# One scatter and one gather moved a step later in a batch, and the opening's identity products sent to another bank

## The reference

```python
x = x + L0_xcond(layernorm(x), ctx, ctx, tau, delta, Wq..bo)   # 16 heads of 16
x = x + L0_ffn(layernorm(x), router, 64 experts, top 8, shared expert)
x = x + L1_xcond(layernorm(x), ctx, ctx, tau, delta, Wq..bo)
x = x + L1_ffn(layernorm(x), router, 8 experts, top 2)

# xcond: scores = (q k^T) * tau + delta; a = softmax(scores / 4); out = (a v) Wo^T + bo
# ffn:   every chosen expert: silu(x Wg) * (x Wu) Wd, times the routing weight, summed per row
```

## Time and profile before

| | us |
|---|---|
| median of 3 runs | 1405.54 |
| lowest and highest run | 1402.01, 1406.44 |
| the profiled execution, its time | 1418.99 |
| its span | 1417.3 |
| PE busy in it | 1272.4 (90% of the span) |
| DVE, ACT, POOL busy | 827.8, 492.7, 557.1 |
| granted TensorE clock, mean | 0.928 |

### The profile page before, as it was taken

The page is one execution under the profiler, slowest core; times in us unless marked ns, Lnnn a source line. Parts: engine busy times, 40 slices in busy tenths (PEclk is TensorE's granted clock), DMA queues, the critical chain, the costliest instruction groups (busy, mean ns, idle before and its releaser), DMA issues. The chain is left out here.

```text
span 1417.3 us, 40365 instructions
## 1 busy us (share of the span) xinstructions
PE 1272.4 (90%) x12838; PEld 980.2 (69%) x12839; DVE 827.8 (58%) x2642; ACT 492.7 (35%) x1255; POOL 557.1 (39%) x706
## 2 busy tenths in 40 slices
PE   5999898999966999999848999999999989999996
PEld 3666565666643788888635666666666779999995
DVE  3467766666746666666445666776676354444442
ACT  1454444344421243344214444444344212212221
POOL 2135555454444101100355655666552223332322
PEclk9999999898977999999967988999899699999998
DMA  4334444335532667875322332333321512533423
GB/s 113 105 110 133 124 131 123 121 115 171 157 118 67 210 201 228 249 221 159 109 76 63 86 87 72 95 90 91 82 68 44 189 40 39 156 93 100 127 66 78
DMA packets 115804, 166.65 MB, mean 118 GB/s; under 512 B 26480, under 2 KB 96768, under 8 KB 114672
## 3 DMA queue, kind: packets, MB, share of 16 engines
q0 software_dynamic: 22672, 58.41, 16.2%
q1 hardware_dynamic: 46496, 54.35, 13.2%
q10 hardware_dynamic: 46560, 52.98, 11.6%
HBM read 87.82 MB, written 63.49 MB: 107 GB/s over the span
## 5 line engine op out<-in xcount | busy, mean ns | idle before, releaser
L1047 DVE TENSOR_REDUCE mx<-banks 112x2 f32<-112x750 f32 x256 | 235.7, 936 | 137.0 <-PE banks L627 111.5
L1894 POOL DMA_INDIRECT xs_d<-xns,idx x160 | 155.1, 969 | 176.6 <-PE banks L651 130.6
L1567 ACT ACTIVATE shared_buf<-banks 125x672 f32<-125x672 f32 x256 | 173.0, 727 | 104.1 <-PE banks L651 94.5
L651 PE MATMUL banks<-attn_buf 18*125 18x112 f32 x3072 | 135.2, 301 | 43.9 <-DVE mx L1047 32.2
L1908 POOL DMA_INDIRECT kept<-y_d,yidx x128 | 123.6, 965 | 119.8 <-issue 91.0
L651 PEld LDWEIGHTS banks<-attn_buf 18*125 18x125 f32 x3072 | 109.8, 198 | 74.3 <-DVE mx L1047 36.7
L919 PEld LDWEIGHTS banks<-xT,attn_buf 128*128 128x128 f32 x1364 | 157.1, 192 | 5.1 <-DVE xT L1433 3.6
L919 PE MATMUL banks<-xT,attn_buf 128*128 128x128 f32 x1364 | 157.4, 275 | 3.3 <-DVE xT L1433 3.3
L864 PE MATMUL banks<-xT,staged 128*128 128x128 f32 x1064 | 142.8, 277 | 6.8 <-DVE staged L1444 6.5
L864 PEld LDWEIGHTS banks<-xT,staged 128*128 128x128 f32 x1064 | 129.1, 192 | 11.5 <-DVE xT L1433 8.1
L627 PE MATMUL banks<-attn_buf 17*112 17x375 f32 x1024 | 123.4, 553 | 7.6 <-ACT shared_buf L1567 7.3
(11 more groups left out here) (214 smaller groups left out, 1957.2 us busy)
## 6 DMA issues: line engine op xcount, KB each, us to landing
shared_buf<-xs_d SPq DMA_DIRECT2D x136, 128.0 KB, 2.5
y_d<-shared_buf ACTq DMA_DIRECT2D x132, 128.0 KB, 2.6
ringbuf<-in_we SPq DMA_DIRECT2D x6, 2176.0 KB, 8.2
ringbuf<-in_we POOLq DMA_DIRECT2D x32, 384.0 KB, 4.7
attn_buf<-attn_buf SPq DMA_DIRECT2D x128, 93.8 KB
attn_buf<-in_ctxT ACTq DMA_DIRECT2D x29, 375.0 KB
xs_d<-zrow ACTq DMA_DIRECT2D x16, 512.0 KB
y_d<-zrow ACTq DMA_DIRECT2D x16, 512.0 KB
```

Source lines behind the costliest of these rows:

```text
L651: last = pe.matmul(bank[SCORES_T[j]][0:KT, t * Q:(t + 1) * Q], kT4[rows, u, i, t * KT:(t + 1) * KT], qT4[rows, u, i, :], start=True, stop= ...
L1047: dve.tensor_reduce(mx[:, i % 2, 2 * p:2 * p + 2], banks[0:Q, 2 * p:2 * p + 2, 0:S], AX.X, ALU.max).then_inc(s_max, 1)
L1567: act.activation(pT[:, slot:slot + 2, :], banks[0:KT, first_bank:first_bank + 2, 0:ST * Q], ACT.Exp, scale=0.25).then_inc(s_exp, 1)
L1894: pool.indirect_dma_start(xs_d[L.number], bass.IndirectOffsetOnAxis(ap=idx[:, b % 2, k:k + 1], axis=0), rows, None).then_inc(s_scat[b % 2] ...
```

## The change

Three edits:

- FILL makes 8 identity products in place of 10, writes bank 4 (the first of the `scores_T` banks) in place of bank 7, and no longer waits for bank 7 to be free.
- In layer 0, POOL's step 0 has one scatter in place of two (k = 2), its step 1 three in place of two (k = 3, 4, 5).
- In layer 1, POOL's step 0 has no gather, its step 1 four in place of three.

```diff
-        FIRST_JOBS = ((... ("ROW1", 0), ("MAX", 0), ("FILL", 10)),
+        FIRST_JOBS = ((... ("ROW1", 0), ("MAX", 0), ("FILL", 8)),
...
                         elif j == "FILL":
-                            for sm, v in free[1]:
-                                wait(pe, sm, v)
-                            idle(r, M1)
+                            idle(r, bank[SCORES_T[0]])
...
                 def body0(n, b):
                     after_scores(n, 0)
                     if in_layer(b, -3):
-                        scatter(L, n - 3, b - 3, 2, 2)
+                        scatter(L, n - 3, b - 3, 2, 1)
                     after_scores(n, 1)
                     if in_layer(b, -3):
-                        scatter(L, n - 3, b - 3, 4, 2)
+                        scatter(L, n - 3, b - 3, 3, 3)
                     if in_layer(b, -1):
                         normalise(1, n - 1, b - 1)
...
                     if in_layer(b, 4):
                         output_row_numbers(b + 4, b % 2)
-                        gather(b + 4, b % 2, 0, 1)
                     after_scores(n, 1)
                     if in_layer(b, 4):
-                        gather(b + 4, b % 2, 1, 3)
+                        gather(b + 4, b % 2, 0, 4)
                     if in_layer(b, -1):
                         normalise(1, n - 1, b - 1)
```

More of the change, by code:

```diff
@@ L318, in build @@
         SP_ATTN, SP_TAB, SP_LATE, SP_PACK, SP_ROWS, SP_LAST, SP_OPEN = (0, 39), (18, 57), 19, 20, 21, (25, 30, 36), 37
-        FIRST_JOBS = ((("K0", 0), ("V2", 0), ("K1", 0), ("XT", 0), ("Q", 0), ("XT", 1), ("V01", 0), ("K0", 1), ("K1", 1), ("ROW0", 0), ("Q", 1), ("BO", 0), ("ROW1", 0), ("MAX", 0), ("FILL", 10)),
+        FIRST_JOBS = ((("K0", 0), ("V2", 0), ("K1", 0), ("XT", 0), ("Q", 0), ("XT", 1), ("V01", 0), ("K0", 1), ("K1", 1), ("ROW0", 0), ("Q", 1), ("BO", 0), ("ROW1", 0), ("MAX", 0), ("FILL", 8)),
                       (("UP3", 0), ("XT", 0), ("Q", 0), ("DOWN3", 0), ("ROW0", 0), ("XT", 1), ("Q", 1), ("ROW1", 0), ("MAX", 0), ("BO", 0)))
```

## The result

| us | before | after |
|---|---|---|
| median of 4 runs | 1405.99 | 1424.93 |
| lowest and highest | 1402.01, 1412.38 | 1419.58, 1426.05 |
| profiled execution, its span | 1417.3 | 1417.9 |
| PE busy in it | 1272.4 | 1280.8 |
| granted clock in it | 0.928 | 0.921 |

The ratio after to before is 1.012, 95% interval 1.0079 to 1.016: the change makes the kernel **slower, by about 17 us**. The forecast was 12 us faster. The two profiled executions have equal spans, because the one of before was slower than each of its four runs (1418.99 against a highest of 1412.38) and the one of after was its fastest. So the profiles are read by place, not by their sum.

The account below looks back on a forecast made before the run. PE was taken to fill the span, so only PE's waits counted. Terms -3.8 (opening), -9.4 (layer 0) and +1.0 (layer 1) gave -12.2 us: 1406.8 profiled, 1393 as run median; range 1382 to 1404.

Parts of the forecast that it names:

- Opening: Start of the program: identity products no longer wait for bank 7, so batch 0's score rows start 3.8 us earlier.
- Layer 0, step 0: Batches 4 to 11: one scatter fewer ends the late signals to DVE; 9.4 us gained, bounds 0 and 9.4.
- the maxima start when DVE is free: Layer 0, batches 4 to 11: DVE's first maxima instruction of step 1 starts 1.2 us earlier, and PE's scores with it.
- Layer 0, step 1. ... Cost nothing: The moved scatter takes 1.25 us ahead of POOL's layer norm chain, covered by 1.71 us of idle time; no cost.
- the rival: Layer 0: third scatter delays step 2's signals; 1409 us, or 1418 if step 1 keeps its stall; chance 0.13.
- the sum: Total of the terms for opening, layer 0 and layer 1: 12.2 us faster, chance 0.40.
- Batch 12: Layer 0: a second scatter lies over the score rows' end, yet the maxima follow without pause; basis for a zero lower bound.
- 1.0 us lost: Layer 1, step 1: the added gather makes xn2 late for PE by 0 to 0.47 us in four batches; middle taken.
- where no row shows that anybody waits for it; I count no gain: Layer 1, step 0: taking the gather out of this step was counted as worth 0 us.
- half clock going away with the pauses: Layer 0, step 1: full clock returns once PE no longer stands, 8.6 us more, 1385 us in all; chance 0.15.

Follow-up runs that it names:

- the written-out loop: Kernel before the change, with DVE's loop over batches 4 to 11 of layer 0 written out except batches 6 and 7; ratio to before 0.9948.
- the three moves of a gather: Against before: fourth gather in step 1 (1.0062), or one gather moved from step 1 to step 0 (1.0085); changed kernel, gather behind layer norm's chain (1.0046 to before).

## Why the prediction was wrong

**Opening: right.** 3.8 us expected, 4.0 by the rows; that products which serve nobody held up the program is shown. Alone it measures 0.9921, 11 us; more than its 4 us, since layer 0's clock was better as well (0.97 against 0.94). How much of that belongs to the edit the profiles can't say, and so the match of 3.8 and 4.0 is one of the rows and not of the ratio.

**Layer 0, step 0: the stall went, its gain did not.** The step "the maxima start when DVE is free" came true. The failed step is the next one, "Layer 0, step 1. ... Cost nothing". I costed the third scatter by its effect on POOL's own chain, and did not put it beside the score rows of step 2, although the rival did exactly that, with the right times. I gave it only 0.13, arguing that a signal at the scatter's end would cost nothing; it came 0.94 us behind that end. PE's wait is 0.86 us at batch 8, not 1.2, so by its waits alone the edit still paid: PE stands 5.9 us less in batches 4 to 11. The second step that failed is the clock, which the sum held as it was: PE is busy 12.7 us longer there, at 0.88 in place of 0.95. Net 365.0 against 365.9, and 1.0038 (0.9990 to 1.0086) alone. Batch 12, my reason for doubt, was no evidence against a scatter as the cause: when the moved scatter stood behind the layer norm's chain, the scatters had all but left the rows' end in steps 0 to 2 of batches 4 to 11, no signal was late there, and the stage ran 19 to 24 us shorter than in before, 9 to 13 shorter than with the opening's edit alone. That is more than the earlier trace rows could give, since the late signals of step 0 went as well, and all half clock of these batches. Why batch 12 was spared is still open, like the odd batches of the written-out loop.

**Layer 1: the largest error.** "1.0 us lost" came from xn2 alone, with bounds 0 and 1.9; the attention went from 387.6 to 404.1 us. On the chip of the forecast this term was nothing: in batches 2 to 13 PE never waits for xn2, before or after. Where nothing else disturbs, it is 5.5 us, above its bound, since PE waits in 11 batches and not in four. The step that failed is "where no row shows that anybody waits for it; I count no gain", and with it that the gather costs nothing at its new place but xn2. PE stands in `scores_T` while a gather is issued, at the old place (2.24 us in place of 0.92 in batch 4, step 1) and at the new one (1.54 in step 2). I had looked for it in no row of layer 1, though I had seen the same coincidence in layer 0. These holds nearly balance; what the move brought is mostly half clock, 8.8 of 11.3 us in batches 4 to 11. That the gather's edit makes the kernel slower is shown by the runs of the parts, and that its loss needs a chip with stalls by the 1.002 on one without; that half clock is the link is read from one profile of before and two of the changed kernel.

**The clock** went against me in both layers. I gave 0.15 to half clock going away with the pauses, named as a point against it that a shifted program may bring half clock elsewhere, and put a price on the first alone.

The range, 1382 to 1404, ended below the measured 1424.93: I had left the one slower rival outside it, and even that one's 1418 had no more than the 1.0 us for layer 1.

## What to carry to other kernels

Before a DMA of POOL is moved, draw where its issue lies against PE's groups, at the old place and the new, in every layer that has such DMAs; each of the three moves of a gather tried here on a chip with stalls freed one meeting and made another. Only the order that took the scatters off the end of the score rows in steps 0 to 2 was worth something. And time a candidate on more than one chip: an edit may buy only what one chip loses.

## What the runs showed of the hardware

- While POOL issues an indirect DMA (0.93 to 0.97 us each in the rows above), on some chips PE's work beside it is held: signals of score rows arrive up to 1.2 us late at DVE, and groups of transposed scores that take 0.92 us take 1.5 to 2.2 at full clock, with pauses of 0.2 to 0.4 us inside them. With 16 rows in place of 112 the pause inside was 0.24 us in place of 0.26.
- On other chips of the same type the same overlap costs nothing: the group takes 0.92 us under a gather of 0.93, the maxima start 0.18 us behind the rows' end under a scatter of 0.94. The whole kernel is 7% faster there, 1312 against 1409 us: fewer stalls and a mean clock of 0.966 in place of 0.928. What tells the chips apart, and by which path POOL holds PE, no run here shows.
- Half clock goes with these holds. In batches 4 to 11 the mean clock is 0.95 and 0.92 (layers 0 and 1) for the kernel before and 0.88 and 0.88 for the changed one. It is 1.00 in both layers for both kernels on chips without stalls, and 1.00 in layer 0 on a chip with stalls where no signal is late.
- A scatter over the rows' end is not enough for a late signal. In step 3 of batches 3 to 14 of before one lies there, and the maxima start 0.18 us behind the rows' end (0.19 in the last two); step 1 of batch 12 is spared, and the odd batches with DVE's loop written out have 0.4 us and not 1.2. What else it takes stays open.
